# Two routed 3x3 convolutions by f16 halves, GpSimd's order of roots and rows, and an earlier first part of the depthwise stage

## The reference, cut to what matters

```
xn     = channel layout of the input, used by a mixture of convolutions
shared = silu(gn(conv1x1(xn)))              # 8 groups
expert = sum over the 2 chosen of 8 experts: weight * silu(gn(conv3x3_e(xn)))
xr     = x + shared + expert                # then a group norm -> xw
q,k,v  = projections of xw; windows of 8x8 pixels, 8 heads
o      = softmax(q k / 4 + bias) v          # per window and head
pe     = depthwise 7x7 conv of v
out    = xr + proj(o + pe)
```

## Time and profile before

| what | us |
|---|---|
| median of three timed runs | 764.08 |
| lowest and highest of them | 758.54, 764.18 |
| the profiled execution | 761.66 |
| its span (first to last instruction) | 759.7 |
| TensorE, VectorE, ScalarE, GpSimd busy | 645.3, 565.1, 453.1, 188.5 |

### The profile page before, as it was taken

One profiled execution on the slowest core, in us unless ns is written; L12 is line 12 of the kernel. 1 busy time (PEld: TensorE's weight loads), 2 busy tenths in 40 slices (PEclk: granted clock), 3 DMA queues, 4 the chain that ended last, 5 costly groups with the idle time before them and its releaser, 6 DMA issues.

```text
span 759.7 us, 18623 instructions
## 1 busy us (share of the span) xinstructions
PE 645.3 (85%) x6926; PEld 388.0 (51%) x6926; DVE 565.1 (74%) x1124; ACT 453.1 (60%) x758; POOL 188.5 (25%) x295
## 2 busy tenths in 40 slices
PE   5426759899989899999999899999999898889892
PEld 3412324655556464656555565646566566444430
DVE  3842656888888888988888888889888977332692
ACT  1123555768676776867686767768676852355451
POOL 4042133140404223131404042231312101000182
PEclk9997868999999999999999999999999999999997
DMA  8433183555646574746556464747452242465194
GB/s 329 180 132 98 59 223 108 174 158 153 184 129 200 145 206 147 213 128 200 160 151 189 128 199 144 215 138 210 134 168 86 82 147 72 139 222 181 20 257 167
DMA packets 53871, 121.13 MB, mean 159 GB/s; under 512 B 10131, under 2 KB 26646, under 8 KB 53782
## 3 DMA queue, kind: packets, MB, share of 16 engines
q1 hardware_dynamic: 41814, 78.87, 32.9%
q0 software_dynamic: 8800, 28.45, 15.3%
q10 hardware_dynamic: 3168, 12.62, 4.3%
HBM read 70.58 MB, written 40.93 MB: 147 GB/s over the span
## 4 chain that ended last, share of the span: by engine, by line
PE 47%; ACT 25%; issue 12%; DVE 6%; DMA 5%; POOL 1%; ACTq 1%; POOLq 1%; SPq 0%; DVEq 0%
PE g L1067 10%; PE g L1085 7%; ACT y L518 6%; PE t L1135 4%; PE g L1095 4%; PE g L1263 4%; ACT vp L563 4%; PE pv L1150 4%; PE s L1124 3%; PE s L1254 3%; DMA vt<-x 3%; ACT y L514 3%; ACT pt L584 3%; PE t L1254 3%; ACT L518 2%
## 5 line engine op out<-in xcount | busy, mean ns | idle before, releaser
L1067 PE MATMUL g<-xsh,wsel 96*128 96x512 f32 x256 | 132.6, 647 | 23.8 <-ACT y L514 13.1
L514 ACT ACTIVATE y<-g 128x512 f32<-128x512 f32 x96 | 55.6, 596 | 92.0 <-PE g L1067 75.6
L875 DVE TENSOR_REDUCE mx<-s 128x8 f32<-128x512 f32 x128 | 87.0, 679 | 26.8 <-PE s L1124 26.8
L811 DVE BATCH_NORM_STATS2 st<-y 128x6 f32<-128x512 f32 x96 | 64.6, 686 | 51.7 <-ACT y L514 51.6
L1135 PE MATMUL t<-ident,less 128*128 128x128 f32 x512 | 79.3, 278 | 15.7 <-ACT pt L584 15.0
L879 DVE TENSOR_TENSOR less<-s,mx 128x512 f32<-128x512 f32 x128 | 88.5, 691 | 4.4
L1067 PEld LDWEIGHTS g<-xsh,wsel 96*128 96x128 f32 x256 | 46.7, 200 | 76.3 <-issue 63.8
L1135 PEld LDWEIGHTS t<-ident,less 128*128 128x128 f32 x512 | 62.5, 145 | 44.7 <-DVE less L879 21.7
L584 ACT ACTIVATE pt<-t 128x512 f32<-128x512 f32 x128 | 74.6, 595 | 14.2 <-PE t L1135 13.7
L1150 PE MATMUL pv<-vp,pt 128*64 128x34 f32 x2048 | 79.2, 222 | 3.0 <-DVE ot L893 2.8
L1150 PEld LDWEIGHTS pv<-vp,pt 128*64 128x64 f32 x2048 | 71.4, 140 | 4.0 <-ACT pt L584 2.9
(11 more groups left out here) (155 smaller groups left out, 1119.7 us busy)
## 6 DMA issues: line engine op xcount, KB each, us to landing
xsh<-xs POOLq DMA_DIRECT2D x64, 210.0 KB, 3.7
xs<-xn ACTq DMA_DIRECT2D x16, 578.0 KB, 2.9
vt<-x SPq DMA_DIRECT2D x4, 2048.0 KB, 17.6
xin<-x POOLq DMA_DIRECT2D x16, 512.0 KB, 4.7
sq_d<-qhl SPq DMA_DIRECT2D x32, 256.0 KB, 2.4
sk_d<-khl SPq DMA_DIRECT2D x32, 256.0 KB, 2.2
stack<-sk_d SPq DMA_DIRECT2D x64, 128.0 KB, 3.5
stack<-sq_d SPq DMA_DIRECT2D x64, 128.0 KB, 2.8
```

The costliest lines, as they stand in the source:

```text
L514: act.activation(y[:, k, h * HALF:(h + 1) * HALF], g[at][:, :], ACT.Identity).then_inc(g_free[at], 1)
L811: last = v.bn_stats(st[:, 2 * k + h, :], y[:, k, h * HALF:(h + 1) * HALF])
L875: v.tensor_reduce(mx[:, p % 2, :], scored, AX.X, ALU.max).then_inc(sem["s_max"], 1)
L1067: last = mm(g[at][:, :], wsel[:, k - 1, C * dy:C * dy + C], xsh[:, k - 1, dy + 16 * h:dy + 16 * h + 16, 0:W], start=(dy == 0), stop=(dy == 1))
```

## The change

- The input of the convolutions is scaled by 16 and split into a high and a low f16 half: ACT writes the normalised image to `vn` in f32 (`normalise`), then its f16 rounding to `xhl[:, 0]` (`high_xn`); GpSimd subtracts (`save_xn`) and issues the save of both halves. ACT does this behind the copy and the q and k halves of p = 0, no longer ahead of them.
- The weights (scaled by 64) are split the same way in the setup: one load, three ACT and two GpSimd operations, and 32 DMAs of SyncE to DRAM. An expert's convolution is then four f16 matmuls per half image (three over 128 partitions, one over 48), the shared one three. `copy_y` scales back.
- GpSimd's step is reordered: `save_xn(b+3)`, `split_v(b)`, `load_weights` x2 (4 DMAs), `rsqrt(b+2, 0, 3)`, `load_rows` x2 (8 DMAs), then as before.
- The first three rounds of the depthwise stage have their taps loaded and split within the last turn, and TensorE runs them between its last steps.

The diff, cut to its core:

```diff
+            sp.dma_start(wx32, wx).then_inc(sem["wx_loaded"], 16)
+            def save_experts():
+                sp.wait_ge(sem["wx_hi"], 2)
+                for copy in range(2):
+                    for e in range(E):
+                        dst = wa_d[e, SHR * copy:SHR * copy + SHR].rearrange("(c d) n -> c (d n)", d=3)
+                        sp.dma_start(dst, wxh[GC * e:GC * e + GC, :]).then_inc(sem["wx_saved"], 16)
+                sp.wait_ge(sem["wx_low"], 2)
+                for e in range(E):
+                    dst = wa_d[e, 2 * SHR:C].rearrange("(c d) n -> c (d n)", d=2)
+                    sp.dma_start(dst, wxl[GC * e:GC * e + GC, 0:6 * C]).then_inc(sem["wx_saved"], 16)
+                    dst = wb_d[e].rearrange("(c d) n -> c (d n)", d=3)
+                    sp.dma_start(dst, wxl[GC * e:GC * e + GC, 6 * C:EXW]).then_inc(sem["wx_saved"], 16)
...
+                if not has1:
+                    for c in range(TAP_RING):
+                        load_taps(c)
...
+            pool.wait_ge(x_loaded[3], 16)
+            for j in range(2):
+                pool.dma_start(xin[:, j, :], x[j].rearrange("c h w -> c (h w)")).then_inc(xin_loaded[j], 16)
+            pool.wait_ge(sem["wx_hi"], 2)
+            nc.gpsimd.tensor_tensor(wxl, wx32[:, 0:EXW], wxh, ALU.subtract).then_inc(sem["wx_low"], 1)
+            nc.gpsimd.tensor_tensor(wsh[:, 1, :], wx32[:, EXW:], wsh[:, 0, :], ALU.subtract).then_inc(sem["wx_low"], 1)
...
+            def save_xn(j):
+                pool.wait_ge(sem["xn_done"], 2 * j + 2)
+                nc.gpsimd.tensor_tensor(xhl[:, 1, 1:H + 1, 1:W + 1], vn[:, :].rearrange("p (y x) -> p y x", x=W),
+                                        xhl[:, 0, 1:H + 1, 1:W + 1], ALU.subtract).then_inc(sem["xn_low"], 1)
+                pool.wait_ge(sem["xn_low"], j + 1)
                 if j > 1:
-                    pool.wait_ge(sem["sum_shared"], j - 1)
-                pool.dma_start(xin[:, j % 2, :], x[j].rearrange("c h w -> c (h w)")).then_inc(xin_loaded[j % 2], 16)
-
-            def load_rows(j):
+                    for k in range(TOP):
+                        pool.wait_ge(rows_loaded[k], ROW_DMAS * (j - 1))
+                pool.dma_start(xs[j % 2], xhl[:, :, :, :].rearrange("p t h w -> p (t h w)")).then_inc(sem["xn_saved"], 16)
+            def load_weights(j, k):
+                if j:
+                    for h in range(2):
+                        wait_ready(pool, f"y{k + 1}", j - 1, h)
+                else:
+                    pool.wait_ge(sem["wx_saved"], 16 * 4 * E)
+                    pool.wait_ge(sem["setup_dve"], 31)
+                e = pool.value_load(rnum[0:1, 4 * j + 2 + k:4 * j + 3 + k], min_val=0, max_val=E - 1)
+                pool.dma_start(wsa[:, k, :], wa_d[bass.ds(e, 1)].rearrange("e p n -> p (e n)")).then_inc(rows_loaded[k], 16)
+                pool.dma_start(wsb[:, k, :], wb_d[bass.ds(e, 1)].rearrange("e p n -> p (e n)")).then_inc(rows_loaded[k], 16)
+            def load_rows(j, k):
                 pool.wait_ge(sem["xn_saved"], 16 * j + 16)
-                for k in range(TOP):
-                    if j:
-                        for h in range(2):
-                            wait_ready(pool, f"y{k + 1}", j - 1, h)
-                    e = pool.value_load(rnum[0:1, 4 * j + 2 + k:4 * j + 3 + k], min_val=0, max_val=E - 1)
-                    size = (H + 2) * WPAD
-                    pool.dma_start(wsel[:, k, :], wx[bass.ds(e, 1)].rearrange("e p n -> p (e n)")
-                                   ).then_inc(sem["chosen_w"], 16)
-                    for s in range(2):
-                        src = bass.AP(xs.tensor, e * (GC * size) + s * WPAD, [[size, GC], [1, 3], [1, RUN]])
-                        dst = xsh[SH // 2 * s:SH // 2 * (s + 1), k, :, :].rearrange("p h w -> p (h w)")[:, 0:RUN]
-                        pool.dma_start(dst, src).then_inc(sem["rows_loaded"], 16)
+                e = pool.value_load(rnum[0:1, 4 * j + 2 + k:4 * j + 3 + k], min_val=0, max_val=E - 1)
+                mine = e * (GC * 2 * PADDED) + j % 2 * (C * 2 * PADDED)
+                def rows(offset, step, count, run):
+                    return bass.AP(xs.tensor, mine + offset, [[2 * PADDED, GC], [step, count], [1, run]])
+                wide = xa[:, k, :, :].rearrange("p h w -> p (h w)")[:, 0:RUN]
+                pool.dma_start(wide[0:SHR], rows(0, 1, 3, RUN)).then_inc(rows_loaded[k], 16)
+                pool.dma_start(wide[SHR:2 * SHR], rows(PADDED, 1, 3, RUN)).then_inc(rows_loaded[k], 16)
+                pool.dma_start(wide[2 * SHR:C], rows(0, 1, 2, RUN)).then_inc(rows_loaded[k], 16)
+                pool.dma_start(xb[:, k, :, :].rearrange("p h w -> p (h w)")[:, 0:RUN2], rows(2, WPAD, 3, RUN2)
+                               ).then_inc(rows_loaded[k], 16)
...
             def step(b, has1, has2, has3):
                 if has3:
-                    load_rows(b + 3)
+                    save_xn(b + 3)
+                split_v(b)
+                if has3:
+                    load_weights(b + 3, 0)
+                    load_weights(b + 3, 1)
                 if has2:
                     rsqrt(b + 2, 0, 3)
                 if has3:
+                    load_rows(b + 3, 0)
+                    load_rows(b + 3, 1)
                     choose_affine(b + 3)
                 if b + 4 < B:
                     load_x(b + 4)
                 if has2:
                     rsqrt(b + 2, 1, 1)
-                if has1:
-                    split_v(b + 1)
-
-            load_x(0)
-            load_x(1)
+            save_xn(0)
+            for k in range(TOP):
+                load_weights(0, k)
+            for k in range(TOP):
+                load_rows(0, k)
             choose_affine(0)
-            load_rows(0)
-            load_rows(1)
+            save_xn(1)
             rsqrt(0, 0, 3)
+            for k in range(TOP):
+                load_weights(1, k)
+                load_rows(1, k)
             choose_affine(1)
             load_x(2)
             rsqrt(0, 1, 1)
+            save_xn(2)
             rsqrt(1, 0, 3)
+            for k in range(TOP):
+                load_weights(2, k)
+                load_rows(2, k)
             choose_affine(2)
-            load_rows(2)
             load_x(3)
             rsqrt(1, 1, 1)
-            split_v(0)
             images(step)
...
+            act.wait_ge(sem["wx_loaded"], 16)
+            act.activation(wx32, wx32, ACT.Identity, scale=WSCALE).then_inc(sem["wx_scaled"], 1)
+            act.wait_ge(sem["wx_scaled"], 1)
+            act.activation(wxh, wx32[:, 0:EXW], ACT.Identity).then_inc(sem["wx_hi"], 1)
+            act.activation(wsh[:, 0, :], wx32[:, EXW:], ACT.Identity).then_inc(sem["wx_hi"], 1)
...
             def normalise(j):
                 act.wait_ge(xin_loaded[j % 2], 16 * (j // 2) + 16)
                 if j == 0:
-                    act.wait_ge(sem["setup_dve"], 9)
+                    act.wait_ge(sem["gn_scaled"], 1)
+                elif j < 3:
+                    act.wait_ge(sem["xn_low"], j)
+                else:
+                    act.wait_ge(sem["v_turned"], j - 2)
+                act.activation(vn[:, :], xin[:, j % 2, :], ACT.Identity, bias=gnx[:, 1, j:j + 1],
+                               scale=gnx[:, 0, j:j + 1]).then_inc(sem["xn_done"], 1)
+            def high_xn(j):
+                act.wait_ge(sem["xn_done"], 2 * j + 1)
+                if j == 0:
                     act.wait_ge(sem["setup_pool"], 1)
-                    sc, sh = gn0[:, 0, 0:1], gn0[:, 1, 0:1]
                 else:
                     act.wait_ge(sem["xn_saved"], 16 * j)
                     for h in range(2):
                         wait_ready(act, "y0", j - 1, h)
-                    sc, sh = gn0[:, 0, j:j + 1], gn0[:, 1, j:j + 1]
-                act.activation(xn[:, 1:H + 1, 1:W + 1], xin[:, j % 2, :].rearrange("p (y x) -> p y x", x=W), ACT.Identity, bias=sh, scale=sc).then_inc(sem["xn_done"], 1)
-
-                act.wait_ge(sem["xn_done"], j + 1)
-                if j:
-                    act.wait_ge(sem["rows_loaded"], 32 * TOP * j)
-                act.dma_start(xs, xn[:, :, :].rearrange("p h w -> p (h w)")).then_inc(sem["xn_saved"], 16)
+                act.activation(xhl[:, 0, 1:H + 1, 1:W + 1], vn[:, :].rearrange("p (y x) -> p y x", x=W),
+                               ACT.Identity).then_inc(sem["xn_done"], 1)
+            normalise(0)
+            for n in range(2):
+                if n:
+                    high_xn(0)
...
+                act.wait_ge(sem["xn_low"], min(b + 3, B))
...
+            def high_taps(c):
+                act.wait_ge(tap_loaded[c % TAP_RING], 16 * (c // TAP_RING + 1))
+                if c >= TAP_RING:
+                    act.wait_ge(sem["dw_ready"], c - TAP_RING + 1)
+                elif c == 0:
+                    act.wait_ge(sem["sum_shared"], B)
+                    for h in range(2):
+                        wait_ready(act, "vt", B - 1, h)
```

(61 more changed lines are left out.)

145 lines of the change are left out of this document (78 added, 67 removed).

## The result

The changed kernel takes 787.75 us in the median (786.4 to 788.56), beside 764.13 of the kernel before on the same chip. The ratio is 1.0316, 95% interval 1.0284 to 1.0348: slower, by 24 us in the medians. The span of the profiled execution went from 759.7 to 786.6 us, by 26.9. Medians are over all timed runs of a kernel; its ratio leaves out executions over 1.5% above its fastest (two of e5's ten, one of e9's four, one of the kernel before).

The account below looks back on a forecast made before the run. TensorE was fullest, VectorE close behind; after the change VectorE would wait for GpSimd's late root. Turns +43, setup -3, the turn after the thirteenth -1, tail -4: +35 us on 761.7, so 797 us; range 765 to 815.

Parts of the forecast that it names:

- the third case: Rival: GpSimd's root is late but TensorE's clock doesn't fall; turn 37.1 us, kernel 784 us; chance 25%.
- From w to E: From the start of `window` on ScalarE (w) to the image's high half from ScalarE's second product (E): 8.86 us.
- From E to the root: GpSimd's operations in a row (its string), from the image's high half to the root's end: 11.05 us, bounds 10.2 and 12.5.
- The wait on VectorE: VectorE idles 3.6 us for GpSimd's root of three columns; 3 to 4 us was named as the sign.
- C: End of `y_coefs` on VectorE, predicted 20.5 us behind the start of `window`, 3.1 later than before.
- From C to w: From the end of `y_coefs` on VectorE to the next `window` on ScalarE: 16.54 us, 0.85 earlier than before.
- The clock: TensorE's clock falls to half behind its wait, while `values` and output projection run: 1.0 us a turn, bounds 0 and 1.8.
- The turn: A steady turn takes 38.1 us, 3.3 longer, bounds 1.4 and 5.5; over 13 turns 43 us, bounds 18 and 72.
- Setup: Work ahead of the steady turns, including the extra load and the weight-split DMAs: -3 us, bounds -8 and +6.
- Tail: Last turn and depthwise stage, three rounds run early on TensorE: -4 us, bounds -7 and +1; fourth round's end -4.8.
- Rival 1: GpSimd's root isn't late, its string under 7.5 us; turn 33.2 us, kernel 733 us; chance 15%.
- rival 2: Root late by no more than the convolutions give, string about 8.7 us; turn 34.8, kernel 754 to 766; chance 8%.

Follow-up runs that it names:

- e5: Changed kernel with GpSimd's subtraction of the image cut from 32 rows to one, order as changed: 765.11 us, ratio 1.0044.
- e9: e3 with the first three depthwise rounds moved back behind the last turn, taps still fetched early: 747.93 us, ratio 0.9821.
- e1: Changed kernel with `split_v` back at the end of the step, as in the kernel before: 748.44 us, ratio 0.9829.
- e6: Changed kernel with 7 unread f16 matmuls of 384 columns in TensorE's gap ahead of the third convolution's first half: 778.62 us, ratio 1.0228.
- after: The changed kernel itself, beside the kernel before: 787.75 us, ratio 1.0316.
- e2: Changed kernel with the loads of the first three tap blocks ahead of `place_v` on SyncE: 785.58 us, ratio 1.0322.
- e3: Changed kernel with `split_v` back at the end of the step and the tap loads ahead of `place_v`: 744.44 us, ratio 0.9774.
- e4: Changed kernel with the root of three columns ahead of the four weight DMAs on GpSimd, `split_v` still ahead of both: 751.79 us, ratio 0.9858.
- e7: e3 with the root also ahead of the weight DMAs on GpSimd: 731.28 us, ratio 0.9625.
- e10: e7 with the first three depthwise rounds moved back behind the last turn, taps still fetched early: 734.04 us, ratio 0.9599.

## Why the prediction was right, point by point

The direction, the place and the main step held: the root is late behind GpSimd's string, and VectorE and TensorE wait for it. 787.75 lies in the range, between the forecast (797) and the third case (784). That it lies nearer to the third case, which has no fall of the clock, is no sign for that case: falls were there in eight of twelve turns, and a string priced too long, a clock priced about right and a tail with the wrong sign added up to it. In part the number is luck. By steps:

- *From w to E.* Predicted w+8.86, measured w+8.75 (the high half lands; GpSimd starts at w+8.83) in every turn without an early fall of the clock. The half convolution was priced at 1.04 and took 1.13.
- *From E to the root.* Predicted 11.05 us with a hand-over of 0.1, measured 9.8 to 10.15 behind it (12.6 in the turn of 43 us, below): late as forecast, but the term was too long by 0.8 to 1.1. Subtraction, save, `split_v` and root have the prices of the sum. What fell away is mainly the first expert's value load (0.64): its first DMA starts at 391.02, where `split_v` ends at 390.97, so the load seems to have lain under the running operation; in e1, where a DMA issue and not a long operation stands ahead of it, the 0.64 are back. A price read from a gap isn't to be added without a look at what runs ahead of it. The rest is smaller: the hand-over to the root (0.15) isn't seen.
- *The wait on VectorE.* Predicted 3.6 us, measured 1.4 in the turns without a fall and 2.1 to 2.4 in most others: under the 3 to 4 named as the sign. The root came 1.2 sooner, and VectorE asked for it at w+17.3, 0.9 later than the w+16.4 of the prediction: its variance was ready at w+16.0 and not w+15.0. That `split_v` also holds up VectorE's small operations (last section) wasn't in the sum; in e1, where it stands elsewhere, VectorE asks at w+16.0.
- *C.* Predicted w+20.5, measured w+19.3, all by the string.
- *From C to w.* Predicted 16.54, measured 16.32. `values` began 0.78 behind C and silu 0.04 behind it, as said.
- *The clock.* Predicted 1.0 us a turn, measured 1.0 to 1.1 in the mean over the twelve turns (seven turns lost 1.5 to 2.4 each against 35.6, 12.8 us in all, without the one of 43 us; about 0.9 of it are later roots). The size was right and the place mostly wrong. I put the fall right behind the long wait, in `values` and the projection. There it lies in three turns (169.17: 3.16 us), and in the other nine they run at full clock (396.84: 1.98 us). In seven turns it lies at the head, in the q and k projection, which is on the way to E, behind gaps of TensorE of 0.6 and 1.30 us. The second gap was not in my sum: the f16 convolution finishes its halves before ScalarE has emptied the bank. e6 closed it and the falls went. That both gaps are needed, the runs suggest: in the twelve turns each of after, e1, e2, e3, e5 and e9 both gaps (0.55 or more, and 1.30) stand 24 times, 17 of them with a fall behind, and the other 48 turns have no early fall; e4 and e7 have only one gap of about 0.8, and none either. That the long wait is needed as well isn't shown. What decides in a given turn stays open: the two stretches of after at 411.79 and 486.59 look alike (1.51 and 1.52 us busy), and the clock falls behind one only.
  The rule of the Trainium skill (TensorE: Matmul & The Clock Gate, "What's actually happening"), that throttled is the default and activity releases it, agrees with e6, where more work made the kernel faster (787.75 to 778.62).
- *The turn.* Predicted 38.1 us, +3.3, measured 37.3, +2.5 in the mean: +0.8 without a fall (forecast for that case: +2.3), about 1.1 by the clock, 0.6 by one turn of 43.09 us. Thirteen turns at 3.3 were 43; twelve at 2.5 are 30, and the thirteenth lies ahead of the third w.
- *Setup.* Predicted -3, measured -4.4 up to the third w, a stretch that holds the thirteenth such turn as well.
- *Tail.* Predicted -4, measured +1.3: the one step with the wrong sign. I followed ScalarE, VectorE and TensorE there and not SyncE. `load_taps` had been put behind `place_v`, which waits for GpSimd's v; ScalarE's tap operation waited 6.47 us with the exponentials behind it. With that order undone the tail is -2.8, against -4; the early rounds give 2 to 3 of the 4.8 us, as measured by e9 and e10.
- *Rival 1* (the root isn't late, 733) and *rival 2* (late by no more than the convolutions give) didn't happen in after. e7 is what rival 1 describes, though by another order and not by a shorter string: 731.28, with C at w+16.5 (said: 16.9) and a turn of 32.88 (said: 33.2).

In the sum +35 was forecast on the span and +26.9 came: 13 too much in the turns, 1.4 too little gain in the setup, 1 of a gain in the fourteenth turn that wasn't there, and 5.3 too little in the tail; 13 + 1.4 - 1 - 5.3 = 8.1. A turn without a fall was priced 1.5 us too long (37.1 against 35.6); 1.1 of it is the string's term.

## What to carry to other kernels

When work is moved onto the emptiest engine, don't ask how busy it is but which short operation of it another engine waits for, and add up everything that now stands ahead of that one in its queue; here a root of 0.9 us stood behind 9 us of string, moving one call out of it gave 39 us back (e1: 787.75 to 748.44), and reordering three calls turned 3% slower into 4% faster (e7). Go through each issuing queue in the same way, SyncE too: a wait placed ahead of a prefetch makes the prefetch late. And if a shortened matmul leaves TensorE in small gaps, look at the granted clock of the stretch behind them before counting the saving.
